# Graph network on one core: GpSimd gathers and scatters every column itself, in place of TensorE lookups and direct sums

## What is computed

```python
def layer0(x):    # two attention layers: softmax over the edges of each dst
    e = leaky_relu(alpha_s[src] + alpha_d[dst]); p = exp(e - segment_max(e, dst)[dst])
    out = segment_sum(h[src] * (p / segment_sum(p, dst)[dst]), dst)
def layer1(x):    # two graph convolutions (gcn_conv)
    out = segment_sum((x @ W)[src] * norm, dst)
def layer2(x):    # sheaf: both ends of each edge get a message
    L = reflections made by a small MLP from (x[src], x[dst])
    out = x - scatter_add(src, coef * (L @ x[dst])) - scatter_add(dst, coef * (L.T @ x[src]))
def layer3(x):    # product: messages from x[dst] and the edge's 8 attributes, summed by src
    m = silu(einsum('ei,ej,ijh->eh', x[dst], edge_attr, W_msg_tp)); agg = segment_sum(m @ W_lin, src)
```

## Time and profile before

| | us |
|---|---|
| median of three runs | 32684.31 |
| the profiled execution | 32672.44 |
| its span | 32670.6 |
| GpSimd busy | 22511.4 (69%), 20275 instructions |
| VectorE busy | 16103.5 (49%) |
| TensorE matmul busy | 13491.3 (41%) |
| ScalarE busy | 2584.3 (8%) |
| DMA queues' share of 16 engines | 7.3% and 6.4% for the two largest |

### The profile page before, as it was taken

The page is one execution under the profiler, slowest core; times in us unless marked ns, Lnnn a source line. Parts: engine busy times, 40 slices in busy tenths (PEclk is TensorE's granted clock), DMA queues, the critical chain, the costliest instruction groups (busy, mean ns, idle before and its releaser), DMA issues. The chain is left out here.

```text
span 32670.6 us, 266258 instructions
## 1 busy us (share of the span) xinstructions
PE 13491.3 (41%) x71326; PEld 10479.5 (32%) x71326; DVE 16103.5 (49%) x34560; ACT 2584.3 (8%) x3901; POOL 22511.4 (69%) x20275
## 2 busy tenths in 40 slices
PE   1111100211110177775777535444444441666663
PEld 1111100211110166664666423232323230454442
DVE  3434429344443677775777534444444443444442
ACT  0000000000000000000000001011111110333330
POOL 5777760477775288885888767777777774777772
PEclk5555555555555588886888756666666665777775
DMA  2111113111112311111111110000000002000001
GB/s 55 16 15 16 16 10 145 22 27 27 27 27 46 111 33 33 33 32 21 33 33 33 25 15 12 14 12 14 12 14 12 14 10 59 18 15 15 15 13 56
DMA packets 1117655, 946.20 MB, mean 29 GB/s; under 512 B 609084, under 2 KB 1060308, under 8 KB 1092308
## 3 DMA queue, kind: packets, MB, share of 16 engines
q1 hardware_dynamic: 468516, 706.27, 7.3%
q0 software_dynamic: 646368, 201.76, 6.4%
q10 hardware_dynamic: 1872, 28.29, 0.2%
HBM read 506.74 MB, written 428.17 MB: 29 GB/s over the span
## 5 line engine op out<-in xcount | busy, mean ns | idle before, releaser
L494 POOL DMA_INDIRECT g1g_G<-tab,g1g_stage x3125 | 3270.3, 1046 | 1237.8 <-issue 1025.7
L494 POOL DMA_INDIRECT se_G<-tab,se_stage x3125 | 3324.5, 1064 | 1085.3 <-issue 1072.5
L494 POOL DMA_INDIRECT g2g_G<-tab,g2g_stage x3125 | 2949.5, 944 | 1272.5 <-issue 1026.4
L1152 POOL DMA_INDIRECT messages<-pe_M,pe_rstage x2625 | 3178.9, 1211 | 905.3 <-issue 817.5
L1152 POOL DMA_INDIRECT messages<-se_M,se_rstage x2625 | 2980.1, 1135 | 865.7 <-issue 799.6
L494 POOL DMA_INDIRECT c2c_G<-tab16b,c2c_stage x2125 | 2769.4, 1303 | 856.0 <-issue 647.3
L494 POOL DMA_INDIRECT c1c_G<-tab,c1c_stage x2125 | 2761.3, 1299 | 793.7 <-issue 647.3
L1053 DVE SCALAR_TENSOR_TENSOR g2gh_junk<-g2gh_pB,g2gh_src_f,earlier 128x128 f32<-128x128 f32 (+4 forms) x2625 | 1453.7, 614 | 1951.3 <-POOLq L493 1928.0
L1567 PE MATMUL se_pTV<-ident,se_pair 128*32 128x128 f32 x3125 | 539.5, 313 | 4159.9 <-DVE se_pair L1474 4159.4
L739 PE MATMUL g1gh_acc<-g1gh_oh_hi,g1gh_oh_lo 128*128 128x100 bf16 x6250 | 539.0, 283 | 3746.7 <-DVE g1gh_oh_hi L719 3746.7
L1065 PE MATMUL g2gh_pB<-ident_b,src_lo 128*128 128x128 bf16 x2625 | 641.4, 286 | 3290.3 <-DVEq L1059 3249.5
(11 more groups left out here) (607 smaller groups left out, 34105.5 us busy)
## 6 DMA issues: line engine op xcount, KB each, us to landing
scans<-g1w_W SPq DMA_DIRECT2D x25, 3187.5 KB, 10.0
c1cm_row<-match SPq DMA_DIRECT2D x500, 128.0 KB, 3.0
c2cm_row<-match SPq DMA_DIRECT2D x500, 128.0 KB, 3.0
edges<-g2g_G SPq DMA_DIRECT2D x25, 2062.5 KB, 6.8
g2w_G<-edges SPq DMA_DIRECT2D x25, 2062.5 KB, 11.6
scans<-g2w_W SPq DMA_DIRECT2D x25, 2062.5 KB, 7.3
g1g_G<-tab,g1g_stage POOLq DMA_INDIRECT x3125, 2.4
g2g_G<-tab,g2g_stage POOLq DMA_INDIRECT x3125
```

The source lines that it names most:

```text
L494: g.indirect_dma_start(out=G[b][:, t, :], out_offset=None, in_=table, in_offset=bass.IndirectOffsetOnAxis(ap=stage[b][:, t:t + 1], axis=0) ...
L1152: g.indirect_dma_start(out=view, in_=M[b][:, DC + t, :], in_offset=None, out_offset=bass.IndirectOffsetOnAxis(ap=stage[b][:, t:t + 1], axis=0)
```

## The change

`Match`, `match_rows` and `DirectSums` are taken out with everything that feeds them. GpSimd gathers all 125 columns of a chunk in `gcn_gather` and scatters all 125 in `sheaf_edges` and `product_edges`. The ranks, the counts in the group and `src_order_scan` cover all columns: `count_in_group` 25 groups a chunk for 21, `count_before_group` 13 and 12 for 11 and 10, scans of 125 elements for 105. The third histogram accumulator (`src_direct`), the additions of `direct` and the waits that tied the stages to the direct sums (`dfree`, `sums.made`) go. The order of the remaining work is kept.

```diff
-DG = 4
-DC = DG * GRP
-SG = NG - DG
-SC = SG * GRP
-LS = NCH * SC
-PC = 40
-PCH = CH - PC
...
 def gcn_gather(...):
                 over_chunks(g, lambda i, b, j: gather_column_loop(
-                    g, i, j, b, table, G, stage, staged, stored, 16, got, PCH))
+                    g, i, j, b, table, G, stage, staged, stored, 16, got))
...
                 def chunk(i, b, j):
-                    match.heat(v, i, 0)
-                    v.wait_ge(stored[b], (j + 1) * 16)
-                    for m in range(max(NB + 1, side.groups)):
-                        if 1 <= m <= NB:
-                            match.mask(v, i, m - 1)
-                        if m + 1 < NB:
-                            match.heat(v, i, m + 1)
-                        if m < side.groups:
-                            side.vector(v, ch, i, side.ranges[0][0] + m)
-                        if 1 <= m <= NB:
-                            match.empty(v, G[b], i, m - 1)
-                    v.wait_ge(match.emptied, (i + 1) * NB + 2)
-                    v.wait_ge(got[b], (j + 1) * (16 * PCH))
+                    for m in range(side.groups):
+                        side.vector(v, ch, i, side.ranges[0][0] + m)
+                    v.wait_ge(got[b], (j + 1) * (16 * CH))
...
 def count_in_group(k, c, name):
-    steps = -(-SG // per)
+    steps = -(-NG // per)
-            landed(group * CH // SG + 1)
+            landed(group * GRP + 1)
...
 def scatter_column_loop(g, i, j, b, view, M, stage, staged, ready, sent, parts=1):
-    for t in range(SC):
+    for t in range(CH):
...
-        g.indirect_dma_start(out=view, in_=M[b][:, DC + t, :], in_offset=None,
+        g.indirect_dma_start(out=view, in_=M[b][:, t, :], in_offset=None,
...
-def match_rows(k, name):
-class Match:
-class DirectSums:
...
 def sheaf_edges(...):
                     def group_step(q, half=None):
...
-                        if half is not None:
-                            spread_column(q, half)
                         evacuate(q)
...
-                with pe.Fori(0, DC // 2) as m:
-                    sums.tensor(pe, NCH - 1, 2 * m, 0)
-                    sums.tensor(pe, NCH - 1, 2 * m + 1, 1)
...
 def src_order_scan(...):
-        G = [c.sb(f"{name}_G{b}", [P, SC, F]) for b in range(2)]
+        G = [c.sb(f"{name}_G{b}", [P, CH, F]) for b in range(2)]
...
 def product_edges(...):
-                    with v.Fori(0, DG + 1) as q:
+                    with v.Fori(0, NG) as q:
                         outer_products(q)
-                    v.wait_ge(silued, i * NG + DG)
-                    v.nop(nofuse=True)
-                    with v.Fori(0, DC // 2) as m:
-                        outer_products(2 * m + (DG + 1))
-                        sums.vector(v, k, M[b], i, 2 * m, 0)
-                        outer_products(2 * m + (DG + 2))
-                        sums.vector(v, k, M[b], i, 2 * m + 1, 1)
...
                 def chunk(i, b, j):
                     a.wait_ge(mfree[b], j + 1)
-                    a.wait_ge(dfree, i + 1)
...
-        half = SG // 2 + 1
+        half = NG // 2 + 1
         aggregate("c1", k.x[:, :, :], tab16, lambda k, c, n: count_before_group(
-            k, c, n, DG, half, k.by_src["start"]))
+            k, c, n, 0, half, k.by_src["start"]))
...
-        vector_block(k, "pj", lambda v, ch: ch(v.tensor_tensor(y[:, :, :], y[:, :, :], direct[:, :, :], ALU.add)))
```

More of the change, by code:

```diff
@@ L708, in vector @@
     def vector(v, ch, i, q, b, landed):
[L709 removed]
+        start, n = steps[q]
         v.wait_ge(used, i * len(steps) + q + 1)
@@ L723, in vector_last @@
         v.wait_ge(used, NCH * len(steps) + 2)
-        for o in range(3):
+        for o in range(2):
             v.tensor_copy(counts[o][:, :], acc[o][:, 0:NT]).then_inc(counted, 1)
@@ L734, in tensor @@
     def tensor(pe, i, q, b):
-        start, n, direct = steps[q]
+        _, n = steps[q]
         pe.wait_ge(ready, i * made[-1] + made[q])
@@ L932, in _, with gcn_gather @@
                 over_chunks(a, chunk)
-def gcn_gather(k, name, table, values, left, scans, carry, side):
+def gcn_gather(k, name, table, scans, carry, side):
     with ExitStack() as st:
@@ L939, in gcn_gather @@
         G = [c.sb(f"{name}_G{b}", [P, CH, D]) for b in range(2)]
-        stage = [c.sb(f"{name}_stage{b}", [P, PCH], I32) for b in range(2)]
+        stage = [c.sb(f"{name}_stage{b}", [P, CH], I32) for b in range(2)]
         staged = [c.sem(f"{name}_staged{b}") for b in range(2)]
@@ L1007, in _, with chunk @@
                     s.sem_inc(stored[b], 16)
-                    load_indices(s, k.src_lanes, stage, staged, b, b, 0, PCH)
-                def chunk(i, b, more=True, index=True):
+                    load_indices(s, k.src_lanes, stage, staged, b, b)
+                def chunk(i, b, more=True):
+                    s.wait_ge(scanned, i + 1)
                     if more:
-                        for m in range(NB):
-                            match.reload(s, i, m)
-                    s.wait_ge(scanned, i + 1)
-                    if index:
-                        load_indices(s, k.src_lanes, stage, staged, i + 2, b, 0, PCH)
+                        load_indices(s, k.src_lanes, stage, staged, i + 2, b)
                     s.dma_start(rows(scans)[:, cols(i), :], G[b][:, :, :]).then_inc(stored[b], 16)
-                for m in range(NB):
-                    match.load(s, 0, m)
                 with s.Fori(0, PAIRS - 1) as j:
@@ L1368, in release_messages, with sheaf_edges @@
 def release_messages(g, b, j, sent, mfree):
-    g.wait_ge(sent[b], (j + 1) * (16 * SC))
+    g.wait_ge(sent[b], (j + 1) * (16 * CH))
     g.nop(nofuse=True).then_inc(mfree[b], 1)
-def sheaf_edges(k, name, table, scans, messages, first, carry, w1, b1, w2, b2, direct, wide):
+def sheaf_edges(k, name, table, scans, messages, first, carry, w1, b1, w2, b2):
     F = D + 1
@@ L1400, in sheaf_edges @@
         pH = c.ps(name + "_pH", [P, 2, 512])
-        sums = DirectSums(c, name + "d", wide)
         staged = [c.sem(f"{name}_staged{b}") for b in range(2)]
@@ L1592, in chunk @@
                     group_step(0)
-                    with pe.Fori(0, DC // 2) as m:
-                        for half in range(2):
-                            group_step(2 * m + (1 + half), 2 * m + half if direct_before else None, half)
-                    with pe.Fori(DC + 1, NG - 1) as q:
+                    with pe.Fori(1, NG - 1) as q:
                         group_step(q)
@@ L1731, in _, with product_edges @@
                     v.tensor_reduce(k.whole[:, :], k.keep_s[:, :], axis=AX.X, op=ALU.min).then_inc(whole, 1)
-def product_edges(k, name, attr, messages, first, w, direct, wide):
+def product_edges(k, name, attr, messages, first, w):
     with ExitStack() as st:
@@ L1751, in product_edges @@
         loaded = [c.sem(f"{name}_loaded{b}") for b in range(2)]
-        dfree, used, step, outered, transposed, copied, product, silued = (
-            c.sem(name + s) for s in ("_dfree", "_used", "_step", "_outered", "_transposed", "_copied",
+        used, step, outered, transposed, copied, product, silued = (
+            c.sem(name + s) for s in ("_used", "_step", "_outered", "_transposed", "_copied",
                                       "_product", "_silued"))
@@ L1826, in chunk @@
                 def chunk(i, b, j):
-                    with pe.Fori(0, DG + 1) as q:
+                    with pe.Fori(0, NG) as q:
                         transpose(i * NG + q)
                         multiply(i * NG + q)
-                    with pe.Fori(0, DC // 2) as m:
-                        for half in range(2):
-                            n = i * NG + 2 * m + (DG + 1 + half)
-                            transpose(n)
-                            sums.tensor(pe, i, 2 * m + half, half)
-                            multiply(n)
-                sums.tensor_first(pe)
                 over_chunks(pe, chunk)
@@ L1909, in program @@
         scan16 = k.dram("scan16", [E + P, D])
-        k.match = [k.dram(f"match{h}", [NCH, PC * P], F16) for h in range(2)]
         k.carried = k.dram("carried", [P + 1, 51])
@@ L2320, in product @@
         spread(k, "pp", k.x, D, tab, first[:, 0:D])
-        product_edges(k, "pe", attr, messages, first, wm, direct, (y, agg))
+        product_edges(k, "pe", attr, messages, first, wm)
         src_order_scan(k, "ps", messages, scan16, carry, D, False)
```

320 lines of the change are left out of this document (54 added, 266 removed).

## The result

The changed kernel takes **34609.6 us** (median of 4 runs, 34601.5 to 34613.6); the kernel before 32686.4 (4 runs, 32668.1 to 32695.0). The ratio is 1.0589, 95% interval 1.0571 to 1.0607. The profiled execution spans 34599.8 us against 32670.6, +1929; the sum said +1777.

What follows compares the result with a forecast made beforehand. GpSimd, going through its columns back to back, was taken to bound all six loops. Terms 736 - 38 + 717 + 200 + 160 + 33 - 31 = +1777 on 32672.4 us gave 34450 us, range about 34170 to 34780.

Steps and rivals of the forecast that it cites:

- the prediction's own sign of being wrong: The forecast is wrong if GpSimd shows waits for semaphores within a stage, or a gap other than 0.305 us.
- The gcn gathers: Both `gcn_gather` stages: 1000 more columns each, one-hots at 0.45 us a group; +736 and +717 us, with -38 in the first.
- Rival A: One-hots and outer products block GpSimd in full: 0.86 us a group, +256 us, `pe_outer` +52; total 34760 us. Chance 0.12.
- The sheaf: 500 more scatters +631 us, the direct sums' excess of 433 goes; +200 us, bounds +150 and +260.
- The product: 500 more scatters +631 us, direct sums -542, `pe_outer` +49, loop gap +20; +160 us, bounds +80 and +250.
- Loop length as the cause of the gap: Loops of 250 gathers show a further issue gap: 77 us taken for a longer gcn loop, 20 us for the product.
- The counting of the second `gat_gather`: 500 more counts, 307 us of VectorE, hidden while it waits for GpSimd: 0 us; if not hidden, 307.
- Rival B: Gathers come out at their floor, one-hots costing nearly nothing: -281 us, 34170 us; without the loop gap 34016. Chance 0.13.
- Rival C: Not slower: GpSimd's 0.305 us issue gap shrinks with less traffic from other queues; 29684 us at zero gap. Chance 0.01.
- Rival D: Another engine becomes the bound, likeliest the sheaf or product group chain at TensorE's lower clock; 35075 us at 1 us. Chance 0.02.
- Rival E: The change doesn't do what it says, the columns being cut elsewhere after all: 32684 us. Chance under 0.01.
- The rule on the shared port: Skill page: some VectorE instructions lock GpSimd out for their whole length; the prediction saw 8.80 us agreeing, scans not.

Runs made afterwards that it cites:

- psum_iota: The changed kernel with the iota that the one-hots are compared with copied to PSUM; 45260 us in one run, against 45055 for the changed kernel on another chip.
- heat_alone: The changed kernel plus 130 unused VectorE compares a chunk in the two gcn stages, sized like the old lookups'; 43151 us against 45055 for the changed kernel.
- best: The kernel before with two semaphores a chunk, iota and the product's one-hot in PSUM; on chip 13, 43145 us against 40754, ratio 1.0598.
- best_2: The same three edits to the kernel before as `best`, run on chip 4; 42511 us against 40404, ratio 1.0537.

## Why the prediction was right, and where its steps were off

The measured 34610 us lies 160 above the 34450 forecast, within the range. The mechanism is the one forecast; 59 us of the difference are the sheaf's and 106 the product's.

- **The bound.** Right where it was measured: six loops with "issue" as their only idle time within a stage, before and after. It is not right everywhere. On chip 4 the same two programs differ by 4683 us, and GpSimd waits within the stages: there the prediction's own sign of being wrong is met.
- **The gcn gathers**, +1418 measured for +1415. The terms hold one by one. "issue" is 1025 us in both. What is left above the floor in `c1c` is 166 us; shared by overlap, 148 belong to 325 groups of one-hots with their compare, 0.455 us each for my 0.45, and 19 to scans. With L the length of an operation and P = 1.25 us the step of a gather, one operation at a random phase costs L^2/2P (it is met with chance L/P and then holds GpSimd for L/2 on average): 0.81^2/2.5 + 0.67^2/2.5 = 0.44 for the pair. That this agrees is in part luck, for the phase is not random: 220 of the 325 pairs cost 0.56 us, as in the rows above, and 62 nothing. And in `g1g` it fails: four one-hots would cost 0.88 us by it and cost 0.52 (328 us over 625 groups). Rival A took the pair as one blocker of 1.48 us; they are two, and GpSimd gets in between: the lengthened gather above ends 0.82 us after the first one-hot and 0.23 after the second, the lengthened scatter 0.82 us after its only blocker.
- **The sheaf**, +259 for +200. The term that was mis-sized is the loop gap, put at nothing with +260 as its bound. It is 25 stops of 2.7 us = 67 us, for the scatters' chunk grew from 105 to 125 columns, past column 113. The two end waits stayed, 67.1 us for 66.1.
- **The product**, +266 for +160. Two terms: the same stop, 67 us for my 20; and `pe_outer`, which holds GpSimd for 173 us, 0.277 each, for my 120. That is the upper bound, which I had worked out by the formula above and then moved away from towards a row (71 us) in which its neighbours shared the blame. Here the formula was the better evidence, on average: 240 of the 625 outer products cost nothing, 377 cost 0.4 to 0.6 us.
- **Loop length as the cause of the gap** was wrong, and that the number came out right for the gathers (77 us forecast, 72 measured) is luck: what the loops of 250 had in common was a chunk of 125 columns on one semaphore.
- **The counting of the second `gat_gather`** at nothing: the stage takes 3978 us before and after. The cover is GpSimd; with it gone, on chip 4, the price was 347 us.
- **The other rivals.** Rival B falls by the 166 us above; what it says against itself, that `g2g`'s counting reads PSUM, was the point (`psum_iota`). Rival C falls: the median gap is 0.305 us in each loop of the changed kernel, with less traffic beside it (DMA share 0.09 in the first `gcn_gather`, 0.16 before). Rival D falls in the first measurements: a product group keeps up with GpSimd at a granted clock of 0.50. Rival E falls: every changed loop has 3125 columns. On the other chips something of D's kind, late VectorE and TensorE, sets the time of most stages, though by pauses and not by the clock: 0.51 in both profiles of the changed kernel.
- **The rule on the shared port.** The earlier trace rows showed 8.80 us beside the compares. `heat_alone` shows the same by the means, 957 to 1174 ns, and `psum_iota` that one PSUM operand is enough to free GpSimd from the one-hots, 1207 to 945 ns. The Trainium skill, page "SBUF — State Buffer", section "SBUF: two separate sides", names these two cases, the two-port mode and the two SBUF inputs. On which instructions block, the trace agrees. The prediction also set the 1.18 us gather among the scans against the rule; that was misread, for the page holds the lock for one instruction, not for a row of them, and a gather that slips in between two scans doesn't contradict it. What a row does is not one thing here: GpSimd came in between scans, between the one-hots of a pair and within rows of 24 one-hots (1.02 us a gather), but not among 26 compares (8.80 us) nor, as the first gather of a chunk, among 100 one-hots (61.14 us).

## What to carry to other kernels

Where GpSimd issues one indirect transfer after another and waits for nothing, a loop's time is its count times the floor, plus what VectorE's operations with two SBUF inputs hold it off: write that sum down before trading VectorE work for columns. Here GpSimd got 2.07 ms of holding back (2642 us above the floor before and 575 after in the four changed loops) and paid 3.76 ms for 3000 columns and 0.28 ms for the stops. L^2/2P was a fair first estimate for an operation that comes now and then; in rows of one-hots it was far off, both ways. When two loops of one kind show a different gap, look at which instruction it falls on before naming a cause. And time a kernel more than once, on other chips too: the sign held, but +5.9% became +11.5%, and on these chips a kernel with GpSimd freed in part lost by it (`best`, `best_2`).

## What the runs showed of the hardware that I had not expected

- The 114th indirect transfer in a row on one semaphore starts about 3 us late (3.00 and 3.38 us in the rows above, where the gap is 0.30 otherwise), in all loops, and not with two semaphores of 63 and 62. What fills up there is not shown.
- In a row of one-hots without a gap GpSimd either falls in step, one gather of 1.02 us for each pair, or, as the first gather of a chunk, stays out for all that is left of the row (60 to 61 us, twelve times a run). What decides between the two is not shown.
- On two chips VectorE, TensorE and ScalarE pause for 12 to 51 us (up to 101 in `g1g`) at points where nothing that the profile shows is missing, only while GpSimd's indirect transfers go out, with the durations of their own instructions unchanged (`se_V` 0.33 us in both). Fewer pauses when GpSimd is held off (`heat_alone`, -1904 us), more when it is freed (`best_2`, +2107). Whether it is the supply of instructions or the signals between engines that is held up, whether the pauses come of the chip, and why the first measurements show none of them, the runs don't tell.
